# A three-phase layer (routed FFN, state-space block, routed FFN): last Silu of the first phase by Tanh, projection products one step earlier, two more pair inputs on GpSimd

## Chip, cores, metric

One core of one Trainium2 chip. The metric is device time in microseconds (us) for one execution, the median of three.

## What is computed

The input is 8 batch rows of 512 tokens with 128 features, all in fp32. Cut to what matters:

```
x = x + 0.5 * ffn(layernorm(x))
x = x + ssm(layernorm(x))
x = x + 0.5 * ffn(layernorm(x))

ffn(x):  every token through 16 experts and 2 shared ones, each silu(x Wg) * (x Wu) Wd;
         the routing weights (4 of 16 experts, within 2 of 4 groups) multiply the 16 outputs
ssm(x):  x, z = split(x W_in); x, z = gelu(conv4(x)), gelu(conv4(z))
         dt, B, C = split(x W_xproj); delta = softplus(dt W_dt + b)
         for each of 16 states n:  h_n[l] = exp(delta A_n)[l] * h_n[l-1] + (delta x B_n)[l]
         y = sum_n C_n h_n + D x;  out = [y, z] W_out
```

## The kernel before

Three phases follow each other on one core: the first FFN (`f1`), the state-space block (`mamba`), the second FFN (`f2`). Each engine has its own hand-written program, with semaphores between them, and each executes its program in order.

**FFN phases.** 144 blocks (8 batch rows times 18 experts). A block is two products of three matmuls each on TensorE (gate, up), the Silu on ScalarE (`act_blocks`), routing weight and gate times up on VectorE (`dve_blocks`, `dve_act`), a high and a low part of the result on ScalarE (`act_hi`) and GpSimd (`act_lo`), and three `pe_down` matmuls four blocks later. When all blocks of the last batch row are done, ScalarE copies the sum out (line 876), TensorE transposes it (line 1242) and VectorE adds it to x (line 1111).

**State-space phase.** The 16 states go two at a time: 8 pairs n for each batch row i, 64 pairs in all, global number g = 8 i + n. One pair is, in the words used below:

- the *spread*: two matmuls copy the rows B of the pair to all partitions, into a PSUM bank (`pe_spread`, line 1862);
- the *input*: VectorE multiplies it by delta x (`dve_input`, line 1772);
- the *decays*: ScalarE computes two Exp (line 1643, into SBUF);
- the *scan*: VectorE, one instruction of 1024 columns (line 1805);
- the *product*: GpSimd multiplies the scan's result by the rows C (line 1527); they come by DMA into `c_ring`, four pairs ahead;
- the *adding*: TensorE adds up the pairs (line 1889, or 1895 in the last batch row), three steps behind.

Scan g waits for the adding of pair g - 4, whose buffer it overwrites (`RING = 4`). The spread of pair g + 1 waits for the end of scan g - 1, whose PSUM bank it takes.

Some pairs are *moved* (`MOVED`): their rows B come by DMA into one of two `b_slots`, GpSimd makes the input (line 1493, `pool_input`), and the decays go to the pair's PSUM bank instead (line 1639), after a *mark*, a matmul of one column (line 1858), says that the bank is free. Before the change, the moved pairs are 6 in batch row 0; 2 and 4 in rows 1 to 5 and 7; 4 in row 6. The DMA loads are in one queue, SyncE's (`load_c`); the first load into a slot waits until all `pe_down` of `f1` are done, since `b_slots` and `act_lo` share memory. So do `states` (two of the four scan buffers) and `act_hi`.

Between the pairs stands the rest of the batch row. At step n = 7 ScalarE copies the transposed x of a later row, loads the Gelu table, computes u and z; TensorE's B/C product (line 1831), delta product (line 1843) and the low part of B (`pe_low`, line 1838) come at n = 0; there ScalarE copies B and C (lines 1583, 1585), computes the Softplus and goes back to the Exp table (`act_delta`). The convolutions (line 1823) stand at n = 1 and 2 for x of row i + 2 and at n = 3 to 6 for z. At n = 3 TensorE transposes y back (line 1902), and at n = 4 it projects out (lines 1911 to 1915). At n = 4 ScalarE applies the layernorm of a later row (line 595, `act_apply`).

`FRONT_ACT`, `FRONT_POOL`, `FRONT_PE` and `FRONT_DVE` say after which pairs a piece of the second FFN's start is put in: layernorm root and shift on GpSimd (lines 564 to 577), and routing of its first row, of which GpSimd compares groups after pair 55 (lines 788 to 798) and VectorE goes on at line 1037, between the input of pair 57 and its scan.

Of the kernel before, what the change touches and what calls it, by code (L numbers as in the profile page):

```python
# [42 lines left out]
MOVED = ((None, 6),) + ((2, 4),) * 5 + ((4,), (2, 4))  # L43
# [34 lines left out]
def program(nc, x_in, w_in, w_xproj, w_dt, b_dt, a_log, d_skip, w_out, k_x, b_x, k_z, b_z,  # L78
            router_w, route_bias, gate_w, up_w, down_w, sh_gate_w, sh_up_w, sh_down_w, out):
    ctx = ExitStack()  # L80
    with ctx:
# [94 lines left out]
        with nc.Block() as block:  # L176
# [32 lines left out]
            @block.scalar  # L209
            def _(ae):  # L210
                f1.act_front(ae)
                head = mamba.act_head(ae)
                for g, _ in enumerate(f1.act_blocks(ae)):
                    if g in (1, 3):
                        setup.act_high_parts(ae, 2 + g // 2)
                    if g == 22:
                        setup.act_selector(ae)
                    if g in (37, 38):
                        setup.act_delta_weight(ae, g - 37, f1.misc)
                    if g == 39:  # L220
# [4 lines left out]
                for g, _ in enumerate(mamba.act_pairs(ae)):  # L225
# [58 lines left out]
FRONT_POOL = (44, 50, 55, 58)  # L284
FRONT_ACT = (46, 48, 50, 52, 54, 56, 61, 62)
# [342 lines left out]
class Ffn:  # L628
# [13 lines left out]
    def __init__(self, nc, ctx, m, p, setup, norm, c_dram, out):  # L642
# [28 lines left out]
        self.stored = sem("stored") if out is not None else None  # L671
        self.spread_ready = sem("spread_ready") if out is None else None
# [235 lines left out]
    def act_blocks(self, ae):  # L908
        nc, m, norm = self.nc, self.m, self.norm
        for i in range(BATCH):  # L910
            for k in range(NE):
                g = i * NE + k
                ae.wait_ge(self.h_ready, g + 1)
                if self.p and g < NSH:
                    pass
                elif k < NSH or self.p == 0 and g < NSH + SPREAD:
                    need(ae, self.act_ready, g - 1)
                    nc.scalar.activation(m["sg"][:, g % 2], self.h_bank[:, g % 2], ACT.Silu
                                         ).then_inc(self.sg_ready, 1)
# [203 lines left out]
    def dve_act(self, dve, g):  # L1123
# [5 lines left out]
        self.nc.vector.scalar_tensor_tensor(m["act"][:, g % ACTS], m["sg"][:, g % 2], 1.0 if g % NE >= NSH else self.HALF,  # L1129
                                            up[:, g % 2], ALU.mult, ALU.mult).then_inc(self.act_ready, 1)  # L1130

    def dve_blocks(self, dve):
        nc, m, norm = self.nc, self.m, self.norm
        routing = self.dve_route(dve, 1, 1)
        for i in range(BATCH):
            for k in range(NE):
# [3 lines left out]
                if k >= NSH:  # L1140
                    w = i * E + e
                    dve.wait_ge(self.sg_ready, g + 1)
# [4 lines left out]
                    else:  # L1147
# [3 lines left out]
                    nc.vector.tensor_tensor(m["sg"][:, g % 2], silu, weight,  # L1151
                                            ALU.mult).then_inc(self.w_done, 1)
# [214 lines left out]
class Mamba:  # L1367
# [80 lines left out]
    def load_c(self, sp):  # L1448
# [3 lines left out]
        for i in range(BATCH):  # L1452
            for n in range(PAIRS):
# [52 lines left out]
    def pool_pairs(self, pool):  # L1506
        nc, m = self.nc, self.m
        for i in range(BATCH):
            for n in range(PAIRS):
# [7 lines left out]
                if i == 0 and n == 4:  # L1517
                    self.pool_input(pool, 0, 1)
# [150 lines left out]
    def act_pairs(self, ae):  # L1669
        self.nc.scalar.preload_act_table_set("exp_and_others")  # L1670
# [10 lines left out]
        for i in range(BATCH):  # L1681
            for n in range(PAIRS):
# [11 lines left out]
                if n == 4 and i + 3 < BATCH:  # L1694
                    self.norm.act_apply(ae, BATCH + i + 3)
# [91 lines left out]
    def dve_pairs(self, dve):  # L1787
# [3 lines left out]
        for i in range(BATCH):  # L1791
            for n in range(PAIRS):
# [10 lines left out]
                if g in (0, RING - 1):  # L1803
                    dve.wait_ge(self.f1.down_done, BLOCKS if g else BLOCKS - 2)
# [158 lines left out]
    def pe_pairs(self, pe):  # L1963
        front = self.front
        for i in range(BATCH):
            for n in range(PAIRS):
                g = i * PAIRS + n
                if 1 < g < ALL_PAIRS - 1:
                    self.pe_spread(pe, g + 1)
                if SUM_LAG <= g <= ALL_PAIRS - PAIRS + 1:  # L1970
# [5 lines left out]
                if step == 0 and i + 1 < BATCH:  # L1976
                    if i == 0:
                        pe.wait_ge(self.f1.acc_read, BATCH)
                    self.pe_bc(pe, i + 1, front[:, 0, :])
                    need(pe, self.z_gated, i)  # L1980
                    self.pe_delta(pe, i + 1, front[:, 1, :])
                if step == LOW_STEP and i + 1 < BATCH:
                    self.pe_low(pe, i + 1, front[:, 0, :])
# [78 lines left out]
```

## Time and profile before

| | |
|---|---|
| median of 3 executions | 863.77 us (863.39 to 864.08) |
| profiled execution | 864.46 us |
| its span, first to last instruction | 862.7 us |
| TensorE busy (matmul) | 833.8 us, 97% |
| VectorE busy | 682.4 us, 79% |
| GpSimd busy | 648.5 us, 75% |
| ScalarE busy | 562.0 us, 65% |
| mean granted clock of TensorE | 0.995 |

Times in the rows below are from the span's start. The first scan begins at 335.30 us and the last at 546.81 us; what stands before and after is FFN. An engine's idle time in brackets stands with the instruction that ended it and with the one that it waited for. Matmul lengths are modelled, and a matmul that is listed with one of twice the length before it started when that one was through; the starts of the next instructions are the better measure.

### The profile page before, as it was taken

How to read it: one execution, taken by the hardware profiler on the slowest of the kernel's cores; microseconds unless marked ns; L12 is line 12 of the kernel's file. 1: busy time of each engine (PE TensorE's matmuls, PEld its weight loads, DVE VectorE, ACT ScalarE, POOL GpSimd, SP SyncE). 2: the span in 40 equal slices, each digit the busy share in tenths (PEclk: the TensorE clock that was granted, in tenths of full speed). 3: DMA queues.
4: the chain of work that ended last, by engine and by line, in shares of the span. 5: the costliest groups of instructions: out<-in, count | busy, mean ns of one | idle time of the engine just before them, and what ended most of it. 6: DMA issues, size and time to landing. Idle time of an engine off the chain costs nothing. (4 is left out here: it accounts for less than half of the span.)

```text
span 862.7 us, 12807 instructions
## 1 busy us (share of the span) xinstructions
PE 833.8 (97%) x3906; PEld 639.7 (74%) x3906; DVE 682.4 (79%) x1264; ACT 562.0 (65%) x1057; POOL 648.5 (75%) x476
## 2 busy tenths in 40 slices
PE   8999999999999999999999998999999999999997
PEld 7678777887877786667666665787887888788885
DVE  6969767776976578999999999787876977776664
ACT  6575565565566657899999894365565556555553
POOL 6958675776685757999999999766776677676765
PEclk9999999999999999999999998999999999999999
DMA  8644474445434242566456554436366436535440
GB/s 216 213 128 115 137 197 109 139 124 157 122 102 129 94 147 98 221 226 216 164 198 226 178 202 148 161 85 180 106 181 175 122 126 159 156 112 174 136 122 25
DMA packets 127286, 130.03 MB, mean 151 GB/s; under 512 B 59497, under 2 KB 83185, under 8 KB 127217
## 3 DMA queue, kind: packets, MB, share of 16 engines
q1 hardware_dynamic: 104512, 123.96, 46.6%
q10 hardware_dynamic: 22704, 5.25, 2.8%
q8 instruction: 31, 0.51, 0.2%
q14 instruction: 39, 0.31, 0.1%
HBM read 119.74 MB, written 9.44 MB: 150 GB/s over the span
## 5 line engine op out<-in xcount | busy, mean ns | idle before, releaser
L817 POOL TENSOR_TENSOR act_lo<-act,act_hi 128x512 fp32r<-128x512 f32 x288 | 372.3, 1298 | 188.7 <-ACT act_hi L928 186.6
L921 ACT ACTIVATE bank<-bank 128x512 f32<-128x512 f32 x252 | 146.8, 582 | 234.0 <-PE bank L1255 224.4
L1151 DVE TENSOR_TENSOR sg<-bank,c_ring 128x512 f32<-128x512 f32 x252 | 172.6, 685 | 97.1 <-ACT bank L921 94.7
L1251 PE MATMUL bank<-x_parts,w_hi 128*128 128x512 f32 x572 | 231.5, 405 | 3.1 <-DVE sg L1151 1.9
L1129 DVE SCALAR_TENSOR_TENSOR act<-sg,bank 128x512 f32<-128x512 f32 x288 | 197.8, 687 | 41.9 <-PE bank L1255 21.1
L1255 PE MATMUL bank<-x_parts,w_hi 128*128 128x512 f32 x572 | 226.0, 395 | 0.0
L1252 PE MATMUL bank<-x_parts,w_lo 128*128 128x512 f32 x572 | 226.0, 395 | 0.0
L928 ACT ACTIVATE act_hi<-act 128x512 fp32r<-128x512 f32 x286 | 178.3, 624 | 0.4 <-PE bank L1227 0.4
L1251 PEld LDWEIGHTS bank<-x_parts,w_hi 128*128 128x128 f32 x572 | 107.4, 188 | 35.9 <-issue 4.8
L1255 PEld LDWEIGHTS bank<-x_parts,w_hi 128*128 128x128 f32 x572 | 107.4, 188 | 26.2
L1252 PEld LDWEIGHTS bank<-x_parts,w_lo 128*128 128x128 f32 x572 | 107.5, 188 | 25.6 <-issue 1.6
L1225 PE MATMUL bank<-act_hi,w_hi 128*128 128x512 f32 x288 | 115.1, 400 | 2.9 <-POOL act_lo L817 2.2
L1226 PE MATMUL bank<-act_hi,w_lo 128*128 128x512 f32 x288 | 113.8, 395 | 0.0
L1227 PE MATMUL bank<-act_lo,w_hi 128*128 128x512 f32 x288 | 113.8, 395 | 0.0
L1527 POOL TENSOR_TENSOR stage<-stage,c_ring 128x1024 f32<-128x1024 f32 x32 | 75.3, 2370 | 6.5 <-DVE stage L1805 6.5
L1527 POOL TENSOR_TENSOR states<-states,c_ring 128x1024 f32<-128x1024 f32 x32 | 75.8, 2375 | 3.0 <-DVE states L1805 3.0
L1225 PEld LDWEIGHTS bank<-act_hi,w_hi 128*128 128x128 f32 x288 | 54.1, 188 | 18.8 <-POOL act_lo L817 4.7
L1643 ACT ACTIVATE stage<-delta,a_neg 128x511 f32<-128x511 f32 x100 | 65.5, 711 | 0.0
L1227 PEld LDWEIGHTS bank<-act_lo,w_hi 128*128 128x128 f32 x288 | 54.1, 188 | 13.2
L1226 PEld LDWEIGHTS bank<-act_hi,w_lo 128*128 128x128 f32 x288 | 54.1, 188 | 13.1 <-issue 0.2
L1823 PE MATMUL bank<-x_pad,w_tap 128*128 128x512 f32 x128 | 61.9, 593 | 0.0
L1772 DVE TENSOR_TENSOR bank<-du,bank 128x1024 f32<-128x1024 f32 x50 | 60.5, 1209 | 0.4 <-PE bank L1862 0.3
(190 smaller groups left out, 1023.7 us busy)
## 6 DMA issues: line engine op xcount, KB each, us to landing
c_ring<-c_dram SPq DMA_DIRECT2D x252, 256.0 KB, 3.6
c_ring<-c_dram SPq DMA_DIRECT2D x64, 512.0 KB, 4.3
b_slots<-c_dram SPq DMA_DIRECT2D x14, 512.0 KB, 4.9
y_dram<-out_t SPq DMA_DIRECT2D x56, 64.0 KB, 2.8
y_tok<-y_dram SPq DMA_DIRECT2D x14, 256.0 KB, 3.7
xt_dram<-xn ACTq DMA_DIRECT2D x40, 64.0 KB, 3.4
xt<-xt_dram ACTq DMA_DIRECT2D x10, 256.0 KB, 3.3
out<-x_sb SPq DMA_DIRECT2D x7, 256.0 KB, 2.3
```

The source lines that it names most:

```text
L817: self.nc.gpsimd.tensor_tensor(m["act_lo"][:, g % LAG], m["act"][:, g % ACTS], m["act_hi"][:, g % LAG].bitcast(FP32), ALU.subtract).then_i ...
L921: nc.scalar.activation(self.h_bank[:, g % 2], self.h_bank[:, g % 2], ACT.Silu).then_inc(self.sg_ready, 1)
L928: nc.scalar.activation(m["act_hi"][:, j % LAG], m["act"][:, j % ACTS], ACT.Copy).then_inc(self.hi_ready, 1)
L1129: self.nc.vector.scalar_tensor_tensor(m["act"][:, g % ACTS], m["sg"][:, g % 2], 1.0 if g % NE >= NSH else self.HALF, up[:, g % 2], ALU.mul ...
L1151: nc.vector.tensor_tensor(m["sg"][:, g % 2], silu, weight, ALU.mult).then_inc(self.w_done, 1)
L1225: nc.tensor.matmul(self.acc, hi, m["act_hi"][:, j % LAG], start=first, stop=False, skip_group_check=True)
L1226: nc.tensor.matmul(self.acc, lo, m["act_hi"][:, j % LAG], start=False, stop=False, skip_group_check=True)
L1227: nc.tensor.matmul(self.acc, hi, m["act_lo"][:, j % LAG], start=False, stop=last, skip_group_check=True).then_inc(self.down_done, 1)
L1251: nc.tensor.matmul(dst, m["w_hi"][:, k, n, :], x_hi, start=True, stop=False)
L1252: nc.tensor.matmul(dst, m["w_lo"][:, k, n, :], x_hi, start=False, stop=False)
L1255: return nc.tensor.matmul(dst, m["w_hi"][:, k, n, :], x_lo, start=False, stop=True)
L1527: product = nc.gpsimd.tensor_tensor(state, state, m["c_ring"][:, 2 * (n % RING):2 * (n % RING) + 2], ALU.mult)
```

## The change

- **Last block of `f1`.** ScalarE loads the Exp/Tanh table right after block 142 and takes Tanh of half the gate instead of Silu for block 143. VectorE multiplies gate by weight meanwhile, and then by tanh + 1, one instruction more; the factor 0.5 goes into `dve_act`. The copy of `act_hi` for block 141 moves ahead of the Tanh. The table load ahead of the first decays goes.
- **Scan buffers.** Even pairs now use `staged`, odd ones `states`; the waits for `pe_down` move from pair 0 to pair 1, and in `f2` the first `act_hi` waits for one adding more.
- **Moved pairs.** Row 0: 5 and 6. Row 6: 2 and 4. All other rows stay at 2 and 4.
- **Products.** B/C and delta products of batch row i + 2 go to n = 7 of row i, `pe_low` ahead of the adding at n = 0.
- **Applies.** `act_apply` from n = 4 to n = 3 (between the copy of y and the moved decays), also the first one of `f2`; the first root of `f2` on GpSimd from pair 44 to pair 38.

```diff
-MOVED = ((None, 6),) + ((2, 4),) * 5 + ((4,), (2, 4))
+MOVED = ((5,6),)+((2,4),)*7
...
-FRONT_POOL = (44, 50, 55, 58)
-FRONT_ACT = (46, 48, 50, 52, 54, 56, 61, 62)
+FRONT_POOL = (38, 50, 55, 58)
+FRONT_ACT = (50, 52, 54, 56, 61, 62)
...
+                elif self.p == 0 and g == BLOCKS - 1:
+                    ae.wait_ge(self.act_ready, g - 1)
+                    ae.wait_ge(self.down_done, g - 1 - LAG)
+                    nc.scalar.activation(m["act_hi"][:, (g - 2) % LAG], m["act"][:, (g - 2) % ACTS], ACT.Copy
+                                         ).then_inc(self.hi_ready, 1)
+                    ae.wait_ge(self.act_ready, g)
+                    ae.wait_ge(self.last_weighted, 1)
+                    nc.scalar.activation(m["sg"][:, (g + 1) % 2], self.h_bank[:, g % 2], ACT.Tanh, scale=0.5
+                                         ).then_inc(self.sg_ready, 1)
...
+                if self.p == 0 and g == BLOCKS - 2:
+                    nc.scalar.preload_act_table_set("exp_and_others")
...
+                    if by_tanh:
+                        product.then_inc(self.last_weighted, 1)
+                        dve.wait_ge(self.last_weighted, 1)
+                        dve.wait_ge(self.sg_ready, g + 1)
+                        nc.vector.scalar_tensor_tensor(m["sg"][:, g % 2], m["sg"][:, (g + 1) % 2], 1.0, m["sg"][:, g % 2],
+                                                       ALU.add, ALU.mult).then_inc(self.w_done, 1)
...
-        return self.staged[:, n - 1] if n in (1, 2) else self.m["states"][:, n // 3]
+        return self.m["states"][:, n // 2] if n % 2 else self.staged[:, n // 2]
...
+                    if i == 0 and n in (1, 3):
+                        self.load_slot(sp, 0, n // 2)
                     if n == 3:
-                        if i == 0:
-                            self.load_slot(sp, 0, 1)
                         self.store_rows(sp, i + 1)
...
-                if i == 0 and n == 4:
-                    self.pool_input(pool, 0, 1)
+                if i == 0 and n in (2, 4):
+                    self.pool_input(pool, 0, n // 2 - 1)
...
+                if n == 3 and i and i + 3 < BATCH:
+                    self.norm.act_apply(ae, BATCH + i + 3)
+                if n == 3 and BATCH - 3 <= i < BATCH - 1:
+                    next(front)
...
+                if n == LOW_STEP and 0 < i < BATCH - 1:
+                    self.pe_low(pe, i + 1, front[:, 0, :])
...
+                if n == 7 and i + 2 < BATCH:
+                    self.pe_bc(pe, i + 2, front[:, 0, :])
+                    pe.wait_ge(self.z_gated, i + 1)
+                    self.pe_delta(pe, i + 2, front[:, 1, :])
```

TensorE at the boundary of two batch rows (here rows 2 and 3), before; from the transposes of n = 6 to the convolution of x at n = 1:

```order
L610 MATMUL bank<-ident,xn 128x128 x4
L1862 MATMUL bank<-bc_parts,sel_n 128x512 x2
L1889 MATMUL bank<-ident,states 128x128 x8
L1862 MATMUL bank<-bc_parts,sel_n 128x512 x2
L1889 MATMUL bank<-ident,stage 128x128 x8
L1831 MATMUL bank<-u,w_bc 64x512
L1843 MATMUL bank<-u,w_delta 128x512
L1838 MATMUL bank<-bc_parts,minus_n 16x512
L1858 MATMUL bank<-stage,ident 128x1
L1889 MATMUL bank<-ident,stage 128x128 x8
L1823 MATMUL bank<-x_pad,w_tap 128x512 x2
```

The same place after (line numbers are those of the changed kernel; 1889 is the spread, 1916 the adding, 1865 `pe_low`, 1885 the mark, 1850 the convolution):

```order
L610 MATMUL bank<-ident,xn 128x128 x4
L1889 MATMUL bank<-bc_parts,sel_n 128x512 x2
L1916 MATMUL bank<-ident,stage 128x128 x8
L1858 MATMUL bank<-u,w_bc 64x512
L1870 MATMUL bank<-u,w_delta 128x512
L1889 MATMUL bank<-bc_parts,sel_n 128x512 x2
L1865 MATMUL bank<-bc_parts,minus_n 16x512
L1916 MATMUL bank<-ident,states 128x128 x8
L1885 MATMUL bank<-stage,ident 128x1
L1916 MATMUL bank<-ident,stage 128x128 x8
L1850 MATMUL bank<-x_pad,w_tap 128x512 x2
```

The two products moved ahead of the spread, from behind the second adding; `pe_low` moved ahead of the adding too. The adding now stands between `pe_low` and the mark.

SyncE's queue at the start of the state-space phase, before (1433 stores the rows B and C of a batch row, 1459 loads C, 1444 loads B of a moved pair):

```order
L1433 DMA c_dram<-bc_rows 32x512
L1459 DMA c_ring<-c_dram 128x1024 x4
L1444 DMA b_slots<-c_dram 128x1024
L1433 DMA c_dram<-bc_rows 32x512
L1459 DMA c_ring<-c_dram 128x1024 x2
L1444 DMA b_slots<-c_dram 128x1024
L1459 DMA c_ring<-c_dram 128x1024 x2
L1444 DMA b_slots<-c_dram 128x1024
```

and after (1457, 1483, 1468 are the same three):

```order
L1457 DMA c_dram<-bc_rows 32x512
L1483 DMA c_ring<-c_dram 128x1024 x2
L1468 DMA b_slots<-c_dram 128x1024
L1483 DMA c_ring<-c_dram 128x1024 x2
L1468 DMA b_slots<-c_dram 128x1024
L1457 DMA c_dram<-bc_rows 32x512
L1483 DMA c_ring<-c_dram 128x1024 x2
L1468 DMA b_slots<-c_dram 128x1024
L1483 DMA c_ring<-c_dram 128x1024 x2
L1468 DMA b_slots<-c_dram 128x1024
```

The loads of C for pairs 2 and 3 now stand behind a load into `b_slots`; one such load more stands in row 0.

GpSimd in batch row 0, before (817 the low parts, 1527 products, 1484 delta x, 1493 inputs):

```order
L817 TENSOR_TENSOR act_lo<-act,act_hi 128x512 x7
L1527 TENSOR_TENSOR states<-states,c_ring 128x1024
L1527 TENSOR_TENSOR stage<-stage,c_ring 128x1024 x2
L1527 TENSOR_TENSOR states<-states,c_ring 128x1024
L1484 TENSOR_TENSOR du<-delta,u 128x512
L1493 TENSOR_TENSOR b_slots<-du,b_slots 128x1024
L1527 TENSOR_TENSOR states<-states,c_ring 128x1024
L1527 TENSOR_TENSOR stage<-stage,c_ring 128x1024 x2
L1493 TENSOR_TENSOR b_slots<-du,b_slots 128x1024
```

and after (818, 1551, 1508, 1517):

```order
L818 TENSOR_TENSOR act_lo<-act,act_hi 128x512 x7
L1551 TENSOR_TENSOR stage<-stage,c_ring 128x1024
L1551 TENSOR_TENSOR states<-states,c_ring 128x1024
L1517 TENSOR_TENSOR b_slots<-du,b_slots 128x1024
L1551 TENSOR_TENSOR stage<-stage,c_ring 128x1024
L1551 TENSOR_TENSOR states<-states,c_ring 128x1024
L1508 TENSOR_TENSOR du<-delta,u 128x512
L1517 TENSOR_TENSOR b_slots<-du,b_slots 128x1024
L1551 TENSOR_TENSOR stage<-stage,c_ring 128x1024
L1551 TENSOR_TENSOR states<-states,c_ring 128x1024
L1551 TENSOR_TENSOR stage<-stage,c_ring 128x1024
L1517 TENSOR_TENSOR b_slots<-du,b_slots 128x1024
L1551 TENSOR_TENSOR states<-states,c_ring 128x1024
```

An input moved in ahead of the product of pair 2; the rest keeps its order.

## Rows read from the trace of the kernel before

**Rows 1.** Batch row 2: stretch, length, busy PE, PEld, DVE, ACT, POOL, clock
```profile
395.60:421.79 26.19, 24.50 (x142) 17.37 (x141) 25.04 (x15) 24.18 (x53) 25.20 (x15) 1.00 0.56 191
```

**Rows 2.** Timeline of VectorE, hand-over and batch row 0: start, length, line, idle before
```profile
335.30 2.29 DVE L1805 TENSOR_TENSOR_SCAN states<-stage,bank 128x1024 f32<-128x1024 f32 x1 [1.82 <-ACT stage L1643]
...
342.13 0.68 DVE L1111 TENSOR_TENSOR x_sb<-x_sb,bank 128x512 f32<-128x512 f32 x1
...
350.04 2.29 DVE L1805 TENSOR_TENSOR_SCAN states<-stage,bank 128x1024 f32<-128x1024 f32 x1 [0.42 <-ACT stage L1643]
...
355.75 2.26 DVE L1805 TENSOR_TENSOR_SCAN stage<-bank,b_slots 128x1024 f32<-128x1024 f32 x1
```

**Rows 3.** Timeline of ScalarE at the hand-over
```profile
332.58 1.28 ACT L1670 ACT_TABLE_LOAD   x1
333.87 1.34 ACT L1643 ACTIVATE stage<-delta,a_neg 128x511 f32<-128x511 f32 x2
```

**Rows 4.** Timeline of TensorE, hand-over to batch row 1
```profile
341.39 0.66 PE L1242 MATMUL bank<-ident,out_t 128*128 128x128 f32 x4 [0.25 <-ACT out_t L876]
...
365.76 0.39 PE L1838 MATMUL bank<-bc_parts,minus_n 128*16 128x512 f32 x1 [0.52 <-ACT bc_rows L1585]
...
367.03 1.88 PE L1823 MATMUL bank<-x_pad,w_tap 128*128 128x512 f32 x4
```

**Rows 5.** Queue of SyncE: first load into a slot
```profile
340.73 0.32 SPq L1444 DMA_DIRECT2D b_slots<-c_dram  x1
```

**Rows 6.** Line 1493, inputs on GpSimd: duration min/median/max
```profile
L1493 POOL TENSOR_TENSOR b_slots<-du,b_slots x14: 2354/2370/2392, 352.2 to 528.2; 128x1024 f32<-128x1024 f32 x14
```

**Rows 7.** Timeline of VectorE, batch row 2
```profile
392.73 2.29 DVE L1805 TENSOR_TENSOR_SCAN stage<-stage,bank 128x1024 f32<-128x1024 f32 x1
395.60 2.29 DVE L1805 TENSOR_TENSOR_SCAN stage<-bank,b_slots 128x1024 f32<-128x1024 f32 x1 [0.59 <-ACT bank L1639]
...
407.10 1.23 DVE L1772 TENSOR_TENSOR bank<-du,bank 128x1024 f32<-128x1024 f32 x1
```

**Rows 8.** Timeline of TensorE, batch row 2
```profile
395.07 0.73 PE L1862 MATMUL bank<-bc_parts,sel_n 128*128 128x512 f32 x2
...
401.45 0.73 PE L1862 MATMUL bank<-bc_parts,sel_n 128*128 128x512 f32 x2
...
406.34 0.71 PE L1862 MATMUL bank<-bc_parts,sel_n 128*128 128x512 f32 x2
```

**Rows 9.** Timeline of ScalarE, batch row 2
```profile
398.61 1.30 ACT L1639 ACTIVATE bank<-delta,a_neg 128x512 f32<-128x512 f32 x2 [1.30 <-PE bank L1858]
...
403.44 1.64 ACT L595 ACTIVATE xn<-x_sb,shift,rstd 128x128 f32<-128x128 f32 x4
```

**Rows 10.** Timeline of GpSimd, batch rows 4 to 7
```profile
453.90 2.37 POOL L1527 TENSOR_TENSOR states<-states,c_ring 128x1024 f32<-128x1024 f32 x1 [0.53 <-DVE states L1805]
...
463.21 2.37 POOL L1527 TENSOR_TENSOR stage<-stage,c_ring 128x1024 f32<-128x1024 f32 x1 [1.04 <-DVE stage L1805]
...
480.09 2.38 POOL L1527 TENSOR_TENSOR states<-states,c_ring 128x1024 f32<-128x1024 f32 x1 [0.54 <-DVE states L1805]
...
503.40 2.36 POOL L1527 TENSOR_TENSOR stage<-stage,c_ring 128x1024 f32<-128x1024 f32 x1 [0.49 <-DVE stage L1805]
...
525.62 0.26 POOL L798 TENSOR_SCALAR g_in<-g_rank 128x16 f32<-128x16 f32 x1
```

**Rows 11.** Timeline of VectorE, last batch row, first instruction behind GpSimd's groups
```profile
525.92 0.23 DVE L1037 TENSOR_TENSOR bank<-bank,g_in 128x64 f32<-128x64 f32 x1
```

**Rows 12.** Last chain of waits, end of the scans: start, length, what
```profile
531.59 2.58 PE bank L1895 x4
...
534.28 1.82 PE bank L1895 x4
```

**Rows 13.** The same view, last batch row; clock is the seventh number
```profile
526.00:528.00 2.00, 1.54 (x10) 1.13 (x8) 1.97 (x3) 2.00 (x5) 2.00 (x1) 0.59 0.33 115
...
532.00:534.00 2.00, 2.00 (x4) 0.77 (x3) 2.00 (x10) 0.00 (x0) 2.00 (x2) 0.70 0.11 18
```

More of the change, by code:

```diff
@@ L224, in _ @@
                 front = f2.act_front_pieces(ae)
-                for g, _ in enumerate(mamba.act_pairs(ae)):
+                for g, _ in enumerate(mamba.act_pairs(ae, front)):
                     if g in FRONT_ACT:
@@ L671, in __init__ @@
         self.stored = sem("stored") if out is not None else None
+        self.last_weighted = sem("last_weighted") if out is None else None
         self.spread_ready = sem("spread_ready") if out is None else None
@@ L922, in act_blocks @@
                                          ).then_inc(self.sg_ready, 1)
-                for j in ([g - 2] if g > 1 else []) + ([g - 1, g] if g == BLOCKS - 1 and self.p else []):
+                for j in ([g - 2] if g > 1 and (self.p or g < BLOCKS - 1) else []) + ([g - 1, g] if g == BLOCKS - 1 and self.p else []):
                     ae.wait_ge(self.act_ready, j + 1)
@@ L926, in act_blocks @@
                     if self.mamba and j in (0, 2):
-                        ae.wait_ge(self.mamba.sum_done, ALL_PAIRS if j else ALL_PAIRS - RING + 1)
+                        ae.wait_ge(self.mamba.sum_done, ALL_PAIRS if j else ALL_PAIRS - RING + 2)
                     nc.scalar.activation(m["act_hi"][:, j % LAG], m["act"][:, j % ACTS], ACT.Copy
@@ L1128, in dve_act @@
         up = self.h_bank if self.p and g < NSH else self.u_bank
-        self.nc.vector.scalar_tensor_tensor(m["act"][:, g % ACTS], m["sg"][:, g % 2], 1.0 if g % NE >= NSH else self.HALF,
+        self.nc.vector.scalar_tensor_tensor(m["act"][:, g % ACTS], m["sg"][:, g % 2],
+                                            self.HALF if g % NE < NSH or self.p == 0 and g == BLOCKS - 1 else 1.0,
                                             up[:, g % 2], ALU.mult, ALU.mult).then_inc(self.act_ready, 1)
@@ L1141, in dve_blocks @@
                     w = i * E + e
-                    dve.wait_ge(self.sg_ready, g + 1)
+                    by_tanh = self.p == 0 and g == BLOCKS - 1
+                    if by_tanh:
+                        dve.wait_ge(self.h_ready, g + 1)
+                    else:
+                        dve.wait_ge(self.sg_ready, g + 1)
                     silu, weight = self.h_bank[:, g % 2], m["c_ring"][:, e % C_SLOTS, :]
@@ L1150, in dve_blocks @@
                     need(dve, self.act_ready, g - 1)
-                    nc.vector.tensor_tensor(m["sg"][:, g % 2], silu, weight,
-                                            ALU.mult).then_inc(self.w_done, 1)
+                    product = nc.vector.tensor_tensor(m["sg"][:, g % 2], silu, weight, ALU.mult)
+                    if by_tanh:
+                        product.then_inc(self.last_weighted, 1)
+                        dve.wait_ge(self.last_weighted, 1)
+                        dve.wait_ge(self.sg_ready, g + 1)
+                        nc.vector.scalar_tensor_tensor(m["sg"][:, g % 2], m["sg"][:, (g + 1) % 2], 1.0, m["sg"][:, g % 2],
+                                                       ALU.add, ALU.mult).then_inc(self.w_done, 1)
+                    else:
+                        product.then_inc(self.w_done, 1)
                     dve.wait_ge(self.w_done, w + 1)
@@ L1667, in act_head, with act_pairs @@
         yield
-    def act_pairs(self, ae):
-        self.nc.scalar.preload_act_table_set("exp_and_others")
+    def act_pairs(self, ae, front):
         ae.wait_ge(self.setup.a_step, 2)
@@ L1693, in act_pairs @@
                     self.act_back_y(ae, i - 1)
-                if n == 4 and i + 3 < BATCH:
-                    self.norm.act_apply(ae, BATCH + i + 3)
+                if n == 4 and i == 0:
+                    self.norm.act_apply(ae, BATCH + 3)
                 if 1 <= i <= 5 and n == 4:
@@ L1802, in dve_pairs @@
                 need(dve, self.sum_done, g - RING + 1)
-                if g in (0, RING - 1):
-                    dve.wait_ge(self.f1.down_done, BLOCKS if g else BLOCKS - 2)
+                if g in (1, RING - 1):
+                    dve.wait_ge(self.f1.down_done, BLOCKS if g > 1 else BLOCKS - 2)
                 nc.vector.tensor_tensor_scan(flat(self.state(g)), flat(decays), flat(added), 0.0, ALU.mult, ALU.add
@@ L1975, in pe_pairs @@
                 step = n if i else n - 2
[L1976 to L1983, printed above, removed]
+                if i == 0 and step == 0:
+                    pe.wait_ge(self.f1.acc_read, BATCH)
+                    self.pe_bc(pe, 1, front[:, 0, :])
+                    self.pe_delta(pe, 1, front[:, 1, :])
+                if i == 0 and step == LOW_STEP:
+                    self.pe_low(pe, 1, front[:, 0, :])
+                if n == 7 and i + 2 < BATCH:
+                    self.pe_bc(pe, i + 2, front[:, 0, :])
+                    pe.wait_ge(self.z_gated, i + 1)
+                    self.pe_delta(pe, i + 2, front[:, 1, :])
                 if i + 2 < BATCH:
```

## Prediction

> **What bounds the kernel now.** A change of 0.2% is 1.73 us here, about what this measurement can tell from none. I read busy time by stretch first. In a batch row of the state-space phase (26.19 us) no engine is idle for long: VectorE is busy 25.04, GpSimd 25.20, TensorE 24.50, ScalarE 24.18 [rows 1]. So whoever is sped up meets the next one within 1 to 2 us, and the question is which wait stands behind each that goes. Then the timelines. VectorE's waits are few: 1.82 us ahead of the first scan, 0.42 ahead of scan 4 [rows 2], some 0.6 per batch row ahead of the moved pair 2, for decays [rows 7]. Counting each of them and each input as gained is the tempting sum. I make the other one, place by place. The profiled execution took 864.46 us, span 862.7; the median is 0.69 lower, and I take what I find off both.
>
> **Hand-over.** The table load takes 1.28 us, and Exp starts 1.29 after it started [rows 3]. The Trainium skill (ScalarE: Activation LUTs, What ACT_TABLE_LOAD costs) adds a drain of about 1.38 us to each switch; by that the saving would be 2.66. The trace shows no drain here, so 1.28. Against it stand the Tanh behind the load and one VectorE instruction of 0.69. The load fills ScalarE from about 330.5 to 331.75, the copy for block 141 to 332.4, the Tanh to 333.0, two Exps (1.34 [rows 3]) to 334.35; VectorE's two instructions end at 334.4. The first scan starts at 334.45: 0.85 earlier than 335.30 [rows 2].
>
> That gain doesn't last. VectorE must add the last row of `f1` at 342.13, and does so when TensorE's transposes (341.39, 0.66 long) are through [rows 2, 4]; their chain (low part, `pe_down`, convolutions, copy) gets only the 0.17 by which block 141's copy comes sooner. Scan 4 hangs on the same chain by ScalarE's decays. Gain at scan 4: **0.17**.
>
> **Row 0, one input more on GpSimd.** VectorE saves 1.21 of work and 1.30 in its cadence. GpSimd gets an instruction of 2.37 [rows 6], 2.33 from start to start. The load for it issues at 340.73 as the first one does now [rows 5]; that one landed 3.6 later, at 344.35, by the view of transfers. Two loads of C that were issued before 333.1 now stand behind it, each some 1.7 of transfer, landing by 346 and 348. GpSimd from 344.35: input 5, products 2 and 3, delta x (1.24), input 6: 4 x 2.33 + 1.24 = 10.56, so 354.9. Scan 6 started at 355.75 [rows 2], so **0.8** is gained there, where VectorE alone could have 1.45.
>
> **Row 1.** ScalarE's next stage starts behind TensorE's transposes of n = 6, which come 0.5 earlier. So `pe_low` goes from 365.76 to some 365.2. But the adding (0.87) now stands between it and the mark; before, it was 1.27 from `pe_low` to the convolution at 367.03 [rows 4], now 2.15. The convolution starts at 367.3, 0.3 later than before, and TensorE is then busy up to the spread of pair 14. Gain at input 14: **0**. The bounds are -0.3 and 0.8.
>
> **Rows 2 to 5.** The apply (1.64 long, 1.54 in cadence [rows 9]) moves into a wait of 1.30 [rows 9]; ScalarE reaches the decays of pair 2 over 1 us sooner, and the 0.59 [rows 7] goes. What is late next is TensorE. From the spread of pair 3, at 395.07, released by the end of scan 17 (392.73 + 2.29), it works without a gap to 401.45, waits 0.1 for scan 19 there, and ends the spread of pair 6 at 407.05 [rows 8]; VectorE's input then starts at 407.10 [rows 7], 14.37 after scan 17 started. Nothing in that stretch is taken off TensorE, since the two products and `pe_low` stood ahead of it. Without the decays' wait that becomes 14.27. VectorE waits 0.7 at that input instead of 0.6 at the scan: **0.1 per batch row**, not 0.6. The gain at input is 0.1, 0.2, 0.3, 0.4 in rows 2 to 5; between scan 2 and that input of each row VectorE is 0.66 further ahead.
>
> The products at n = 7 wait for u and z; u comes about 4.9 ahead of scan 1, the products take 1.8, the next spread is through at -2.6 and is wanted at -1.3. `pe_low` at -1.8 lets the convolution end at 2.15 behind the start of scan 1, when TensorE needs it at 2.34. Priced at nothing, cover 0.2.
>
> **Row 6.** The moved pair takes another 1.30 off VectorE, where TensorE has slack: 0.4 + 1.3 = 1.7 for VectorE before pair 55. GpSimd has to take 2.33 more.
>
> **GpSimd, to the groups.** It is idle for lack of a scan ahead of pairs 35, 38, 43 and 50: 0.53, 1.04, 0.54, 0.49 [rows 10]. From pair 35's start at 453.90 to the end of the groups, 525.62 + 0.26 = 525.88, that is 71.98 with 2.07 idle in it. VectorE's line 1037, in front of scan 57, starts at 525.92 [rows 11]: 0.04 behind, so it hangs on GpSimd now. After the change the idle time goes and the input comes: 71.98 - 2.07 + 2.33 = 72.24. Pair 35 is 0.2 + 0.66 = 0.86 earlier, at 453.04, so groups end at 525.28. **Gain 0.6**; VectorE gets there 1.7 sooner and waits 1.1. How early could it be? Without any wait from 344.35, GpSimd reaches pair 35 at 452.5 (four batch rows of 24.6, one with a root of 2.8, less what is done by then), and the groups end at 524.7: 1.2 is the most that all of the edits together can give here. The least, with pair 35 nowhere earlier than it was, is -0.3.
>
> **The end of the scans.** From scan 57 on the chain is TensorE's, without a gap into `f2`, so what is gained there arrives. But its clock is at half there: 0.59 in 526 to 528, 0.70 in 532 to 534 [rows 13], 1.2 GHz for some 6.5 us after it had been waiting for scans. An adding that takes 1.82 at 2.4 GHz took 2.58 partly at the lower level [rows 12]; three instructions together lose about 2.5. I leave that 2.5 as it is. First phase and `f2` are TensorE's and unchanged; the one adding more that `f2` waits for is done by 549, wanted at 552.3: nothing.
>
> Sum: 0.6 us. 863.77 - 0.6 = **863.2 us**; the profiled execution would be 863.9.
>
> **Rivals.**
> 1. *The clock falls for longer.* Ahead of scan 57 VectorE now waits 1.1 for GpSimd, and TensorE, which has nothing to do until that scan ends, idles nearly 3 us instead of 1.1. If the half clock lasts 2 to 4 us longer into the chain that starts at the end of scan 57, it costs half of that, 1 to 2: 864.2 to 865.2, net 0.4 to 1.4 slower than before. It turns the sign from 0.6 of extra loss on. For it: the fall happened after such waits. Against: in those 6.5 us it came back by 534 with TensorE busy from the end of scan 57 on. By the Trainium skill (TensorE: Matmul & The Clock Gate, HAM oscillation) each idle stretch between bursts can cost a new fall. This trace agrees, 0.59 after the waits.
> 2. *The clock comes back sooner*, since the fall too moves ahead: 1.2 to 2.5 of the 2.5 saved, 860.7 to 862.0. Same rows, other phase.
> 3. *VectorE bounds it after all*: its waits and inputs all count, 0.85 + 0.42 + 0.9 + 4 x 0.59 + 2 x 1.30 = 7.1, so 856.7. Against it the two sums above, of TensorE and GpSimd.
> 4. *GpSimd starts late*: the load lands at 6 instead of 3.6 us, or loads of C hold up products 2 or 6. Its sum moves up by 2, no idle time catches it, less the 0.6 of slack at pair 35: 864.6. The same time comes if the products at n = 7 don't do what they are moved for (`pe_low` later by 0.9).
>
> **Chances.** Forecast (gain between 0 and 1.2, clock as before) 0.57; rival 1 0.15, a third of it beyond +1.73; rival 2 0.14, nearly all beyond -1.73; rival 3 0.05; rival 4 0.09, of which 0.03 beyond. Faster by over 0.2%: 0.18. Slower: 0.08. Within: 0.74. The range reaches from the middle of rival 2 to the end of rival 1, 861.2 to 865.2; it leaves out rival 3 and the tails.
>
> **What would show it.** Right: first scan near 334.5, but the add of line 1111 still near 342; in rows 2 to 5 no wait at the decays of pair 2 but 0.6 to 0.7 ahead of the input of pair 6, released by the spread, and the batch row still at about 26.1; GpSimd without idle time from pair 43 to the groups; line 1037 waiting about 1 us for line 799. Wrong: batch rows of 25.5, line 1037 with no wait, GpSimd idle ahead of pairs 43 or 50, or a stretch of half clock of another length than some 6.5 us near 530.

## The result, and the profile after

The changed kernel takes **865.79 us**, median of 18 runs (864.65 to 866.92), beside 864.07 for the kernel before in the same comparison: ratio 1.0020, 95% interval 1.0014 to 1.0026. So it is 1.7 us slower, where 0.6 faster was predicted, and 0.6 above the predicted range, which ended at 865.2. The profiled execution took 866.55 with a span of 864.8 (before 864.46 and 862.7).

VectorE at the hand-over and in row 0 (start, duration, engine, line, operation, tiles, and in brackets the idle time before it with its releaser), to be held against [rows 2]:

```profile
333.14 1.10 DVE L1173 SCALAR_TENSOR_TENSOR sg<-sg 128x512 f32<-128x512 f32 x1 [1.08 <-ACT sg L928]
334.28 0.69 DVE L1141 SCALAR_TENSOR_TENSOR act<-sg,bank 128x512 f32<-128x512 f32 x1
334.88 2.28 DVE L1832 TENSOR_TENSOR_SCAN stage<-stage,bank 128x1024 f32<-128x1024 f32 x1
342.42 0.69 DVE L1123 TENSOR_TENSOR x_sb<-x_sb,bank 128x512 f32<-128x512 f32 x1 [0.64 <-PE bank L1266]
350.39 2.29 DVE L1832 TENSOR_TENSOR_SCAN stage<-stage,bank 128x1024 f32<-128x1024 f32 x1 [0.46 <-ACT stage L1667]
355.70 2.29 DVE L1832 TENSOR_TENSOR_SCAN stage<-bank,b_slots 128x1024 f32<-128x1024 f32 x1 [0.82 <-POOL b_slots L1517]
```

The first scan comes 0.42 sooner (0.85 forecast), mostly because line 1173 took 1.10 instead of 0.69. Scan 4 is 0.35 *later*: block 143's `dve_act` (line 1141) starts at 334.28, before the change at 332.78, and TensorE's chain behind it is late too (the add of the last row at 342.42 instead of 342.13). Scan 6 starts as before, where 0.8 sooner was forecast.

GpSimd in row 0, against [rows 5, 6], and ScalarE's table load with the copy behind it, against [rows 3]:

```profile
345.05 2.36 POOL L1517 TENSOR_TENSOR b_slots<-du,b_slots 128x1024 f32<-128x1024 f32 x1 [1.87 <-DMA b_slots<-c_dram]
362.02 2.35 POOL L1551 TENSOR_TENSOR stage<-stage,c_ring 128x1024 f32<-128x1024 f32 x1 [1.73 <-DMA c_ring<-c_dram]
```

```profile
330.40 1.28 ACT L960 ACT_TABLE_LOAD   x1
331.69 0.63 ACT L924 ACTIVATE act_hi<-act 128x512 fp32r<-128x512 f32 x1
```

TensorE in row 1, against [rows 4]. The adding (line 1916) now runs between the low part (line 1865) and the mark:

```profile
365.82 0.39 PE L1865 MATMUL bank<-bc_parts,minus_n 128*16 128x512 f32 x1 [0.46 <-ACT bc_rows L1609]
366.05 1.03 PE L1916 MATMUL bank<-ident,states 128*128 128x128 f32 x8
366.92 0.28 PE L1885 MATMUL bank<-stage,ident 128*128 128x1 f32 x2
367.06 1.07 PE L1916 MATMUL bank<-ident,stage 128*128 128x128 f32 x8
...
380.83 0.71 PE L1889 MATMUL bank<-bc_parts,sel_n 128*128 128x512 f32 x2
```

From low part to convolution it is 2.15, as forecast, but the low part is not sooner than before (365.82 beside 365.76). The convolution starts at 367.97 instead of 367.03, the spread of pair 14 at 380.83 instead of 380.16, and VectorE's input 14 is 0.67 late (381.58 instead of 380.91).

A steady row: VectorE, and the stretch from one scan 2 to the next by engine (columns: stretch, length, busy time and instructions of PE, PEld, DVE, ACT, POOL, granted TensorE clock, DMA share, GB/s), against [rows 1, 7]:

```profile
407.73 1.23 DVE L1799 TENSOR_TENSOR bank<-du,bank 128x1024 f32<-128x1024 f32 x1 [0.68 <-PE bank L1889]
421.75 2.26 DVE L1832 TENSOR_TENSOR_SCAN stage<-bank,b_slots 128x1024 f32<-128x1024 f32 x1
```

```profile
395.60:421.75 26.15, 24.29 (x142) 17.31 (x141) 24.93 (x15) 24.37 (x53) 25.69 (x16) 1.00 0.56 193
```

The wait at the decays of pair 2 is gone, the one for the spread of pair 6 stands in its place, and the row still takes 26.15, as predicted.

GpSimd around pair 38 and at the groups, then VectorE ahead of scan 57, against [rows 10, 11]:

```profile
463.78 2.36 POOL L1551 TENSOR_TENSOR stage<-stage,c_ring 128x1024 f32<-128x1024 f32 x1 [1.00 <-DVE stage L1832]
...
527.29 0.26 POOL L799 TENSOR_SCALAR g_in<-g_rank 128x16 f32<-128x16 f32 x1
```

```profile
521.72 2.29 DVE L1832 TENSOR_TENSOR_SCAN stage<-stage,bank 128x1024 f32<-128x1024 f32 x1
...
527.59 0.23 DVE L1049 TENSOR_TENSOR bank<-bank,g_in 128x64 f32<-128x64 f32 x1 [2.46 <-POOL g_in L799]
...
527.99 2.28 DVE L1832 TENSOR_TENSOR_SCAN states<-stage,bank 128x1024 f32<-128x1024 f32 x1
```

VectorE starts scan 56 at 521.72 instead of 522.50 and waits 2.46 for GpSimd, whose groups end at 527.55 instead of 525.88. Scan 57 is 1.67 late, scan 63 1.75. This is where the kernel got slower. Before the change VectorE came out of its input 57 only 0.03 after the groups, and did not wait:

```profile
524.70 1.21 DVE L1772 TENSOR_TENSOR bank<-du,bank 128x1024 f32<-128x1024 f32 x1
```

The end of the scans by stretch, against [rows 13]:

```profile
524.00:526.00 2.00, 1.94 (x12) 1.74 (x13) 1.12 (x2) 1.46 (x3) 1.92 (x3) 0.71 0.02 8
...
532.00:534.00 2.00, 2.00 (x4) 0.77 (x3) 2.00 (x5) 0.00 (x0) 2.00 (x2) 0.50 0.31 123
534.00:536.00 2.00, 2.00 (x7) 0.99 (x6) 2.00 (x8) 0.00 (x0) 2.00 (x2) 0.73 0.20 78
```

The granted clock is at half (1.2 of 2.4 GHz) for some 10 us, from about 524.8 to 535, instead of 7.

### The profile page after: what moved, and what is told of

Its sections match the earlier page's. It is cut to its first block and busy times, and to the rows that moved or that the text cites. A ratio compares the mean times of both kernels' runs of the same rounds, so it can differ in the third digit from the quotient of the medians.

```text
span 864.8 us, 12815 instructions
## 1 busy us (share of the span) xinstructions
PE 833.0 (96%) x3906; PEld 639.6 (74%) x3906; DVE 680.5 (79%) x1263; ACT 562.2 (65%) x1057; POOL 652.5 (75%) x478
## 5 line engine op out<-in xcount | busy, mean ns | idle before, releaser
L1832 DVE TENSOR_TENSOR_SCAN states<-stage,bank 128x1024 f32<-128x1024 f32 x31 | 70.8, 2285 | 2.9 <-PE bank L1916 0.6
L1667 ACT ACTIVATE stage<-delta,a_neg 128x511 f32<-128x511 f32 x96 | 62.8, 708 | 0.0
```

## The experiments

Executions differ by up to 1.8 us in where the state-space phase begins. So the table counts from the start of one VectorE instruction of the first phase (`dve_act` of block 140), which stands at 324.38 before and 324.31 after and which none of the edits touches. Times are in us, each from one profiled execution. "Scan" columns are starts, "groups" is the end of GpSimd's line 799. The ratio is to the kernel before in runs on the same chip, with its 95% interval. The medians come from several chips, on which the kernel before took 863.58 to 864.07, so kernels of different groups are compared by their ratios.

```
kernel                     scan 4    14     38  groups     57     63   median   ratio
before                      25.66  57.85 136.40 201.50 201.94 222.43  864.07
after                       26.08  58.59 137.04 203.24 203.68 224.25  865.79  1.0020 (1.0014-1.0026)
a1 all pairs as before      26.08  58.87 137.32 202.37 202.81 222.47  864.09  1.0004 (0.9995-1.0013)
a2 row 0 as before          26.11  58.91 137.37 203.65 204.09 224.95  866.35  1.0029 (1.0018-1.0040)
a3 row 6 as before          26.09  58.59 137.05 202.09 202.54 223.05  863.91  1.0002 (0.9993-1.0011)
a4 Silu as before           25.66  58.53 136.99 203.23 203.67 224.60  865.75  1.0020 (1.0011-1.0030)
b1 low part behind adding   26.07  58.28 136.72 202.96 203.40 223.20  865.59  1.0018 (1.0009-1.0027)
b2 row 1's order as before  26.09  57.97 136.41 202.63 203.07 224.39  864.96  1.0011 (1.0002-1.0021)
b3 root as before           26.06  58.56 137.02 203.86 204.30 224.49  865.65  1.0021 (1.0013-1.0030)
b4 routing step later       26.09  58.59 137.03 203.23 200.88 224.58  866.05  1.0023 (1.0013-1.0034)
c1 = a3 + b2                26.07  57.98 136.43 201.45 201.88 221.53  863.10  0.9992 (0.9984-1.0001)
c2 row 7 one pair           26.10  58.60 137.06 201.00 201.44 222.20  863.24  0.9997 (0.9988-1.0006)
c3 = c2 + b2                26.07  57.98 136.43 200.35 200.79 221.55  862.62  0.9993 (0.9984-1.0002)
c4 before, row 6 two        25.66  57.86 136.39 203.96 204.40 224.05  866.08  1.0034 (1.0022-1.0047)
d1 = c3 + a2                26.10  58.53 136.99 200.88 201.32 222.09  863.37  0.9991 (0.9981-1.0000)
d2 = c3 + a4                25.66  57.92 136.38 200.32 200.77 221.53  862.30  0.9981 (0.9973-0.9990)
d3 = c2 + all rows' order   26.11  58.07 136.62 201.03 201.47 222.24  863.48  0.9996 (0.9987-1.0005)
d4 = c3 + a2 + a4                                                     862.32  0.9976 (0.9967-0.9986)
e1 = d4                     25.65  57.83 136.27 200.21 200.65 221.42  862.69  0.9985 (0.9976-0.9994)
e2 = c3                     26.08  58.20 136.66 200.56 201.01 221.78  862.59  0.9989 (0.9978-0.9999)
```

**First four: each part of the change undone alone.**

```diff
 a1 +MOVED = ((None, 6),) + ((2, 4),) * 5 + ((4,), (2, 4))
 a2 +MOVED = ((None, 6),) + ((2, 4),) * 7
 a3 +MOVED = ((5, 6),) + ((2, 4),) * 5 + ((4,), (2, 4))
 a4 -  Tanh, line 1173, the early table load;  + Silu in place, load in act_pairs
```

a1: 

> The table of moved pairs as before the change (pair 6 of row 0, pair 4 of row 6), all else as changed. Theory (GpSimd bounds: two more inputs of 2.33 us each on it, and a late start): without them GpSimd is again idle ahead of pairs 35 and 38, the routing groups end near 525 instead of 527.6, line 1049 starts near 525.0 to 525.9, and the kernel is 1.7 to 2.7 us faster than the changed one, 863.1 to 864.1. Rival A (the hand-over with Tanh costs it): gives 0.3 back at most, still 865.5 or more. Rival B (products for B, C and delta at n = 7, applies at n = 3): the same, still above 865.5.

a2: 

> Only row 0 as before: pair 6 alone moved, pair 5 back on VectorE; row 6 keeps two moved pairs. Theory: GpSimd has 2.33 us less work in row 0 and does not wait 1.73 for the C of pair 6; pair 35 starts about 1 us sooner than 454.5, as far as scans let it, groups end near 526.6, the kernel is 0.7 to 1.2 us faster than the changed one: 864.6 to 865.1. If the late start alone were the cause: 1.7 faster. If row 0 did not matter: 865.8.

a3: 

> Only row 6 as before (pair 4 alone moved), row 0 keeps pairs 5 and 6. Theory: GpSimd is without idle time from pair 38 on, so its input of 2.33 us counts in full: groups end near 525.3, line 1049 no later than before the change, the kernel 1.5 to 2.3 us faster than the changed one: 863.5 to 864.3. If row 0 is the whole cause: 865.8, no change.

a4: 

> The last Silu of the first phase and its table load as before, the rest as changed. Theory: the copy of the last row leaves TensorE 0.3 sooner (340.75 instead of 341.08), the load for row 0 with it, GpSimd starts 0.3 sooner, and the kernel is 0 to 0.35 us faster than the changed one: 865.4 to 865.8. Rival A (the hand-over is the cause): 1 to 1.7 us faster. If the Tanh form were worth its 0.42 at the first scan: 0.4 slower, 866.2.

a1 and a3 took the time that was expected, and in the median nearly the whole loss is gone (1.0004, 1.0002). Their groups are a miss: 2.2 to 2.5 sooner was expected, and they end 0.87 and 1.15 sooner. In both, GpSimd waits 1.1 for scan 50 again, which has one input more ahead of it on VectorE. GpSimd in a3:

```profile
504.93 2.36 POOL L1551 TENSOR_TENSOR stage<-stage,c_ring 128x1024 f32<-128x1024 f32 x1 [1.10 <-DVE stage L1832]
```

From there VectorE and GpSimd reach line 1049 together, as before the change, so the input of 2.33 that GpSimd loses is worth only 1.15.

a4 changes nothing at the end, as expected. a2 was a miss: it is not faster but 0.4 *later* at scan 57. GpSimd's late start in row 0 and its wait of 1.73 are made up by idle time ahead of pair 38 (1.59 in a2, 1.00 in the changed kernel), which is released by scan 38.

**Second four: the order in row 1, the root, the wait.**

```diff
 b1  pe_pairs, n == 0:  -pe_low; pe_add_states   +pe_add_states; pe_low
 b2  pe_pairs, g == 8:  +pe_bc(2), pe_delta(2), pe_low(2) behind pe_add_states; none at g == 7
 b3 -FRONT_POOL = (38, 50, 55, 58)
    +FRONT_POOL = (44, 50, 55, 58)    and the two applies on ScalarE back to pairs 46 and 48
 b4 -FRONT_DVE = {54: 2, 56: 1, 57: 1, 58: 1, ...}
    +FRONT_DVE = {54: 2, 57: 1, 58: 2, ...}
```

b1: 

> At n = 0 of rows 1 to 6 TensorE does the adding first and the low part behind it, as before the change; the products for B, C and delta stay at n = 7. Theory (in row 1 the adding of 0.87 that now stands between low part and convolution makes the spread of pair 14 0.67 late, and VectorE keeps that for good): the convolution in row 1 starts near 367.5 instead of 367.97, scan 14 comes 0.2 to 0.5 sooner, scan 38 too, and the kernel is 0.2 to 0.5 us faster than the changed one: 865.3 to 865.6. Rival (that loss is made up later, in GpSimd's waits): no change.

b2: 

> Only row 1 has its products for row 2 and the low part back behind the adding of n = 0, as before the change; rows 2 to 6 as changed. Theory: input 14 comes where it was before the change (0.65 sooner than in the changed kernel), scans 14, 22, 38 and 57 all 0.5 to 0.7 sooner, routing groups near 526.9, and the kernel 0.5 to 0.7 us faster than the changed one: 865.1 to 865.3. Rival: if GpSimd's own sum from row 0 on sets the end, no change, 865.8.

b3: 

> The first root of the second feed-forward phase on GpSimd back at pair 44, and its applies on ScalarE back at pairs 46 and 48; all else as changed. Theory: the root in the wait-free stretch is the same 2.8 us, but GpSimd then waits about 0.5 for scan 43 that it does not wait for now; the groups end 0 to 0.6 later than 527.55 and the kernel is 0 to 0.6 us slower than the changed one: 865.8 to 866.4. Rival (the early root causes the loss): 1.7 us faster, 864.1.

b4: 

> The step of the routing that waits for GpSimd's groups (line 1049) is put behind scan 57 instead of ahead of it, with the next one behind scan 58. Theory: scan 57 no longer waits 2.46 for GpSimd, it starts 1.9 to 2.5 sooner, TensorE idles less ahead of it, and the kernel is 1.2 to 2.5 us faster than the changed one: 863.3 to 864.6. Rival (the wait only moves: scan 58 then hangs on the same groups, or the last product of pair 63 on GpSimd ends it): less than 0.5 faster.

b2 met its numbers at the scans: input 14 is back where it was, and scans 14, 38 and 57 come 0.6 sooner. Its trace gains nothing at scan 63, where the granted clock is at half from 528.3 on for 6.8 us (more below), and its ratio, 1.0011, has an interval that overlaps that of the changed kernel. TensorE in b2, row 1, with mark and convolution close behind the low part again:

```profile
365.04 0.39 PE L1865 MATMUL bank<-bc_parts,minus_n 128*16 128x512 f32 x1 [0.63 <-ACT bc_rows L1609]
365.27 0.28 PE L1885 MATMUL bank<-stage,ident 128*128 128x1 f32 x2
365.41 1.07 PE L1916 MATMUL bank<-ident,stage 128*128 128x128 f32 x8
366.31 1.88 PE L1850 MATMUL bank<-x_pad,w_tap 128*128 128x512 f32 x4
```

b1 gives half of that at scan 14 (0.31). b3: no difference in the median, although VectorE is 3.1 *later* at scan 56 there (200.49 on this count, 197.41 in the changed kernel). The groups, and scan 57 with them, are only 0.6 later: most of VectorE's lateness goes into its wait of 2.46 for them.

b4 is the most instructive, and a miss for the forecast: the rival that was named held. Scan 57 starts 2.8 sooner, and nothing is gained. VectorE, then TensorE in b4:

```profile
524.82 2.29 DVE L1832 TENSOR_TENSOR_SCAN states<-stage,bank 128x1024 f32<-128x1024 f32 x1
527.20 0.23 DVE L1049 TENSOR_TENSOR bank<-bank,g_in 128x64 f32<-128x64 f32 x1
```

```profile
529.54 1.98 PE L1922 MATMUL bank<-stage,ident 128*128 128x512 f32 x4 [0.34 <-POOL stage L1551]
...
534.16 3.64 PE L1922 MATMUL bank<-states,ident 128*128 128x512 f32 x4 [2.52 <-POOL states L1551]
```

The wait of VectorE (2.46) becomes one of TensorE (2.52) for the product of pair 57, which stands behind the same groups on GpSimd (this trace has two short falls of the clock, at 524.1 and 534.3). It is GpSimd's queue that bounds here, not one wait for it.

**Third four: one input less on GpSimd at another place, and both causes removed.**

```diff
 c1  a3 and b2 together
 c2 +MOVED = ((5, 6),) + ((2, 4),) * 6 + ((None, 4),)
 c3  c2 and b2 together
 c4  the kernel before, with  +MOVED = ((None, 6),) + ((2, 4),) * 7
```

c1: 

> Row 6 with one moved pair, and row 1 with its products for row 2 behind the adding of n = 0, both as before the change; row 0 keeps two moved pairs, Tanh, and the order of rows 2 to 6 stay as changed. Theory (two causes that add up: the input of row 6 on GpSimd, 1.7 to 1.9, and the order in row 1, 0.65 to 0.8): scans 55 and 57 come 0.6 sooner than in the kernel with row 6 alone as before, and the kernel takes 863.0 to 863.4, 0.5 to 0.9 less than that one and about 0.6 less than the kernel before. Rival (TensorE's chain from scan 57 on or its clock takes it back): 863.9.

c2: 

> Pair 2 of row 7 is not moved any more, only pair 4 is; rows 0 to 6 as changed. GpSimd so has one input less ahead of pair 55 and the routing groups, VectorE one more of 1.30, behind them. Theory (GpSimd's queue from pair 38 to the groups and to the product of pair 57 sets the end, and VectorE has 2.46 to spare there): groups end near 525.3, the product of pair 57 is 2.3 sooner, scan 57 hangs on VectorE again, and the kernel is 1.2 to 2.2 us faster than the changed one, 863.6 to 864.6. Rival (VectorE's work is what counts): 0.5 to 1.3 slower.

c3: 

> The same, and the order of row 1 as before the change. Theory: 0.5 to 0.8 below the kernel without that edit, 863.0 to 863.9, below the kernel before. Rival: no difference between the two, where VectorE has no part in the end any more.

c4: 

> The kernel before the change with one edit: row 6 moves pairs 2 and 4 instead of 4 alone. Theory: GpSimd's queue from pair 38 on is longer by 2.33 less what it waits for scans 43 and 50 (1.03), groups end 1.3 to 2.3 later than 525.88, VectorE waits there for them, and the kernel is 1.0 to 2.0 us slower than before, 864.8 to 865.8, although VectorE has 1.3 less work. Rival (VectorE or TensorE bounds there): no change or up to 1.3 faster.

c2 takes one input from GpSimd ahead of the groups and gives it to VectorE behind them: the groups come 2.24 sooner, nearly the whole 2.33, scan 57 too, and 2.05 is left at scan 63. VectorE in c2, to compare with the 2.46 above:

```profile
525.33 0.23 DVE L1049 TENSOR_TENSOR bank<-bank,g_in 128x64 f32<-128x64 f32 x1 [0.20 <-POOL g_in L799]
```

c1 and c3 are 0.6 to 0.7 below a3 and c2 from scan 14 to scan 57 (at scan 63 too for c3; a3's trace loses 0.9 more to the clock there): the two causes add, and in c1, without either, the groups end at 201.45 beside 201.50 before the change. The medians of c2 and c3 lie 0.4 below their expected ranges, which were counted from 865.79; on this chip the kernel before took 863.58 instead of 864.07. c4 got slower, but for a reason that was not written down, and by more (2.5 at scan 57). VectorE in c4:

```profile
504.25 2.29 DVE L1805 TENSOR_TENSOR_SCAN stage<-bank,b_slots 128x1024 f32<-128x1024 f32 x1 [3.72 <-ACT bank L1639]
...
529.18 0.23 DVE L1037 TENSOR_TENSOR bank<-bank,g_in 128x64 f32<-128x64 f32 x1
```

Scan 50 waits 3.72 for decays. On ScalarE these stand behind the copies of row 7's products, for which it waits 1.35, and behind an apply of `f2`. GpSimd then waits 0.76 for scan 50, and line 1037 does not wait at all. So c4 says nothing on GpSimd's queue. It suggests what the moved products and applies are needed for beside a second moved pair in row 6: in b3, where only the applies and the root are back, scan 50 waits 1.40 for its decays.

**Last six: are the other parts worth anything once GpSimd is relieved?**

d1: 

> From the kernel with pair 4 alone in row 7 and row 1's order as before: row 0 back to pair 6 alone. Theory (scan 14 is set by TensorE's chain in row 1, so nothing of row 0 lasts): scans 14, 22 and 57 stay within 0.1, the kernel stays at 862.6, +-0.3. If row 0's input were worth its forecast 0.8: 863.4.

d2: 

> From the same kernel: the last Silu and its table load as before the change. Theory: scan 0 comes 0.35 later, scan 4 0.42 sooner, and neither lasts beyond scan 14: 862.6, +-0.3. If the late scan 4 reached the end: 862.2. If the early first scan did: 863.0.

d3: 

> From the same kernel: TensorE's order of the products and the low part as before the change in all rows, not in row 1 alone; ScalarE's applies stay moved. Theory (the moved products bring 0.03 to 0.1 per row): 0 to 0.4 slower, 862.6 to 863.0. If the order costs in rows 2 to 6 as it does in row 1: up to 0.6 faster, 862.0.

d4: 

> From the same kernel: row 0 back to pair 6 alone and the last Silu as before, together. Theory: 862.6, +-0.3, as each alone. If they add up: the sum of the two differences.

e1: 

> Pair 4 alone in row 7, row 1's order as before, row 0 back to pair 6 alone and the last Silu as before. If Tanh costs time at the end: scan 14 comes 0.4 sooner than in the kernel with Tanh and pair 6 alone (58.53 behind block 140's act), at 57.9 to 58.1, and the ratio stays near 0.998. If not: scan 14 at 58.5, ratio 0.999.

e2: 

> With Tanh and two moved pairs in row 0, row 7 with pair 4 alone, row 1's order as before. If Tanh costs time even where scans 14 to 63 stand at the same places as without it: ratio 0.9990 or more on the chip on which the other runs at 0.998. If the difference was one of the calls: both at the same ratio within 0.0006.

The profiled execution of d4 was disturbed (3192 us), so its trace is not used; e1 is the same kernel again. With row 1's order as before, scan 14 stands at

```
              one moved pair in row 0     two
Tanh          58.53 (d1)                  57.98, 58.20 (c3, e2)
Silu          57.83 (e1)                  57.92 (d2)
```

and the differences last to scan 63 (222.09; 221.55, 221.78; 221.42; 221.53). By these traces Tanh costs 0.7 with one moved pair, and the second pair wins back 0.3 to 0.5 of that and nothing without Tanh. They are single executions, and c3 and e2, one and the same kernel, are 0.2 apart. That "nothing of row 0 lasts", as expected for d1, was wrong. In the times the two kernels that ran side by side, e1 and e2, can't be told apart (0.9985 and 0.9989), so that Tanh costs anything in the median is not shown. d2 and d4 stayed in their ranges. d3, the order as before in all rows, costs 0.1 at scan 14 and 0.7 at scan 57; its median of 863.48 is above the 863.0 that was allowed, but by the ratios (0.9996, 0.9993) it can't be told from c3.

Two of these kernels are faster than the kernel before by their intervals, by 0.15 to 0.24%: d2 (0.9981) and e1 (0.9985; 0.9976 as d4). For e2 (0.9989, up to 0.9999; 0.9993, up to 1.0002, as c3) it is not clear.

## Why the prediction was wrong

The sum hung on one number, the end of GpSimd's groups, and rightly so: a1, a3 and c2 move the kernel with it, and b4 shows that it is the queue. (In b3 it is 0.6 later and the median does not show it.) That number was forecast 0.6 *sooner* than before and came 1.74 later, counted as in the table: 2.34 apart. In its steps:

- **"After the change the idle time goes", 71.98 - 2.07 + 2.33: the step that failed, 1.6 of the 2.34.** Of the 2.07 taken out, 1.04 stood ahead of pair 38, for scan 38 [rows 10], and the prediction gave VectorE only 0.3 at that place. A GpSimd that is 0.86 earlier waits longer there, not less; it waited 1.00, and 0.59 to 1.61 in the other runs. No head start at pair 35 gets past scan 38. By the prediction's own rows it should have been: pair 38 0.3 sooner, then 62.67 - 1.03 + 2.33. That is groups 1.0 *later*, and the sign turns.
- **"Gain at input 14: 0": the second step, 0.94.** It measured -0.67, and scan 38 came 0.64 late instead of 0.3 sooner. The mechanism (2.15 from low part to convolution instead of 1.27) was priced right; wrong was that TensorE's transposes would come 0.5 sooner and carry the low part with them. They came 0.06 later, and scan 6, 0.8 sooner in the forecast, stood where it was. The worst bound was -0.3; b2 shows 0.6 for this step alone. It is also why VectorE is 0.7 sooner at scan 56 on the table's count, and not 1.7.
- From pair 38 to the groups it measured 63.77, where 62.67 - 1.03 + 2.33 = 63.97. So +0.64 + 1.10 = 1.74, the whole of scan 57's delay.
- "0.04 behind, so it hangs on GpSimd now" was a misreading: before the change VectorE had no idle time there, and both engines came to line 1037 within 0.03. The sum does not rest on it, but a sooner end of the groups by itself would have gained nothing there.
- *Hand-over*: sign wrong at scan 4 (-0.35 for +0.17). Line 1173 was costed at 0.69, from an instruction with one input in PSUM; it has both in SBUF and took 1.10. a4 shows that in the changed kernel this costs nothing at the end.
- *Row 0*: GpSimd's first input started 0.7 later than forecast, and it waited 1.73 for the C of pair 6, whose load stood in the queue behind a slot's load that waits for scan 5. Rival 4 had both, at 864.6, which is half of the loss; but its "no idle time catches it" is what a2 refutes, so the loss did not come from there.
- *Rows 2 to 5*: right in mechanism, and in size near enough: from scan 14 to scan 38 the kernel gained 0.1, where three rows at 0.1 each were forecast. It was right too that VectorE's 1.3 in row 6 goes into a wait.
- *The clock*: a half clock of 10 us instead of 7 did come, as in rival 1, but it is not the loss. It began at 524.8, ahead of TensorE's wait of 2.79 for scan 57, and lasted through it. From scan 57 to 63 it took 20.49 before, 20.57 after, and 19.66, 19.65 and 19.65 in a1, c1 and c4, where the clock stays at 1.00:

```profile
526.00:528.00 2.00, 1.83 (x17) 1.59 (x16) 1.97 (x4) 1.88 (x4) 1.83 (x4) 1.00 0.55 205
528.00:530.00 2.00, 0.55 (x2) 0.48 (x3) 2.00 (x6) 1.16 (x3) 2.00 (x2) 1.00 0.00 0
```

  (a1, by stretch.) So the fall costs 0.8 and 0.9 in these two traces, not the 2.5 that was read off three instructions; probably because VectorE's scans stand beside them. Elsewhere it depends on where the fall lies: 19.80 in b1, where it takes 3.4 us, 21.32 in b2. That is why the column for scan 63 must be read with care. Nor do the medians owe their difference to the clock: its mean is 0.996 over the 18 executions of the changed kernel, and 0.996 over the 140 of the kernel before beside the experiments. It is 0.998 to 0.999 in a1, c1, c2 and c3, so some of what these gain in the median may be the clock's. c4 has the full clock from scan 57 on and has the highest ratio.

Left open: why the second moved pair in row 0 helps only beside Tanh, what of the 0.7 of d3 belongs to which row, and what the moved applies do by themselves. A load for row 1 put behind the C of pair 6 was not tried.

## What to carry to other kernels

Idle time on an engine is not a reserve by itself: each piece has a releaser (the instruction that it waits for). Work put in ahead of a piece can fill it, but an earlier start cannot carry past it. So sum from the last idle piece that stays, with its releaser's own gain, and not from an earlier one. And a wait moved off one engine is a gain only if the engine that was waited for has nothing else queued that the end needs: b4 took a wait of 2.46 from VectorE and got it back as 2.52 on TensorE.

## What was not expected of the hardware

A `scalar_tensor_tensor` of 128x512 fp32 with both inputs in SBUF (line 1173, one instruction) took 1.10 us, and 0.69 with one of them in PSUM (line 1141, 288 of them, mean 687 ns). The Trainium skill has this (Vector Engine (DVE) Microarchitecture Reference, Points that are easy to get wrong): two SBUF sources that are not bf16 halve its throughput. The trace agrees in direction: 0.41 more, 1.6 times the length and not twice.

The Trainium skill also adds a drain of some 1.38 us to a table load (ScalarE: Activation LUTs, What ACT_TABLE_LOAD costs). At the new place too, the trace shows none: load at 330.40, next instruction at 331.69.
